# Two query units made in turn, and the count tables merged and loaded earlier, in a one-core graph layer

## The reference

```python
xn = _layernorm(x)                                   # x is 1250 x 1024
x = x + gnn(xn, W, a, src, dst) + mix(xn, w_ql, w_qr, w_key, w_value)
x = x + ffn(_layernorm(x))                           # 8 experts, the best 2 of each row

# gnn: 20000 edges
h = x @ W;  al = h @ a_l;  ar = h @ a_r
e = exp(-leaky_relu(al[src] + ar[dst]))
h_prime = segment_sum(e[:, None] * h[dst], src) / (segment_sum(e, src) + EPS);  elu(h_prime)
# mix
query = (x @ w_ql) * (x @ w_qr)
linear_attn = query @ (key.T @ value)                # key = x @ w_key, value = x @ w_value
```

## Time and profile before

| | us |
|---|---|
| median of 3 runs | 1197.39 |
| the three runs | 1197.3, 1197.39, 1201.2 |
| the profiled execution | 1201.76 |
| its span | 1199.7 |
| PE busy | 1153.2 (96%) |

### The profile page before, as it was taken

One profiled execution on the slowest core, in us unless ns is written; L12 is line 12 of the kernel. 1 busy time (PEld: TensorE's weight loads), 2 busy tenths in 40 slices (PEclk: granted clock), 3 DMA queues, 4 the chain that ended last, 5 costly groups with the idle time before them and its releaser, 6 DMA issues.

```text
span 1199.7 us, 15119 instructions
## 1 busy us (share of the span) xinstructions
PE 1153.2 (96%) x5588; PEld 987.2 (82%) x5588; DVE 586.4 (49%) x1171; ACT 308.7 (26%) x416; POOL 469.8 (39%) x394
## 2 busy tenths in 40 slices
PE   6999999999999999999999989999967999999996
PEld 5898888888788999999978868888855888788884
DVE  7935766655332122211023457978589622644444
ACT  2422112133120221211021223333353411523232
POOL 0003557457787567500000016324323444434343
PEclk9999999999999999999989999999968999999998
DMA  9382875773534445355476653462288954885753
GB/s 356 111 341 53 236 206 115 240 178 51 124 45 43 92 93 118 88 115 117 97 191 186 233 164 112 154 251 102 102 299 295 342 102 92 244 246 121 195 86 72
DMA packets 115835, 192.15 MB, mean 160 GB/s; under 512 B 33960, under 2 KB 63912, under 8 KB 114624
## 3 DMA queue, kind: packets, MB, share of 16 engines
q1 hardware_dynamic: 81008, 159.53, 38.5%
q0 software_dynamic: 34768, 31.82, 19.4%
HBM read 136.19 MB, written 61.68 MB: 165 GB/s over the span
## 4 chain that ended last, share of the span: by engine, by line
PE 80%; DVE 9%; DMA 8%; issue 1%; ACT 1%; SPq 0%; DVEq 0%; POOL 0%; ACTq 0%; POOLq 0%
PE ps L1562 25%; PE ps L1563 25%; PE ps L1564 25%; DMA xm<-in_x 6%; DVE e_lo L1387 2%; PE ps L1781 2%; PE ps L1710 2%; PE ps L1650 1%; DMA gx<-xn_d,tok_of 1%; DVE xn_lo L1114 1%; DVE stats L1086 1%; DVE xm L1311 1%; DVE acc L1102 1%; PE ps L1608 1%; SPq L623 0%
## 5 line engine op out<-in xcount | busy, mean ns | idle before, releaser
L731 POOL DMA_INDIRECT cnt_d<-times,addr_i x160 | 263.2, 1645 | 179.2 <-DMA cnt_d<-times,addr_i 96.5
L1562 PE MATMUL ps<-e_hi,lt_hi 128*128 128x512 f32 x368 | 147.3, 400 | 2.8 <-DVE e_lo L1387 1.9
L1564 PE MATMUL ps<-e_hi,lt_lo 128*128 128x512 f32 x368 | 143.6, 390 | 0.0
L1563 PE MATMUL ps<-e_lo,lt_hi 128*128 128x512 f32 x368 | 143.4, 390 | 0.0
L1563 PE MATMUL ps<-xt_lo,q_hi 128*128 128x416 f32 (+1 forms) x384 | 135.0, 352 | 0.0
L1562 PE MATMUL ps<-xt_hi,q_hi 128*128 128x416 f32 (+1 forms) x384 | 134.9, 351 | 0.0
L1564 PE MATMUL ps<-xt_hi,q_lo 128*128 128x416 f32 (+1 forms) x384 | 134.7, 351 | 0.0
L840 POOL DMA_INDIRECT out<-y,row_put x46 | 74.2, 1613 | 86.7 <-ACT y L1044 49.2
L1562 PEld LDWEIGHTS ps<-e_hi,lt_hi 128*128 128x128 f32 x368 | 69.1, 188 | 23.3 <-DVE e_lo L1387 9.2
L1255 DVE TENSOR_TENSOR qs<-ps,qs 128x416 f32<-128x416 f32 (+1 forms) x24 | 14.2, 592 | 143.4 <-PE ps L1564 143.4
L1562 PE MATMUL ps<-h_hi,att_hi 128*128 128x512 f32 (+1 forms) x200 | 79.6, 398 | 3.7 <-issue 3.7
(11 more groups left out here) (257 smaller groups left out, 2384.4 us busy)
## 6 DMA issues: line engine op xcount, KB each, us to landing
e_raw<-in_L_ffn_expert_W SPq DMA_DIRECT2D x64, 512.0 KB, 9.4
cnt_d<-zeros SPq DMA_DIRECT2D x20, 640.0 KB, 12.8
rows<-key_d SPq DMA_DIRECT2D x8, 1250.0 KB, 7.3
acc<-in_x SPq DMA_DIRECT2D x18, 512.0 KB, 7.8
w_raw<-in_L_mix_w_key SPq DMA_DIRECT2D x16, 512.0 KB, 3.8
cnt_d<-cnt_d POOLq DMA_DIRECT2D x10, 640.0 KB, 7.5
cnt<-cnt_d SPq DMA_DIRECT2D x10, 640.0 KB, 6.5
h_d<-hs SPq DMA_DIRECT2D x18, 256.0 KB, 2.0
```

The costliest lines, as they stand in the source:

```text
L731: nc.gpsimd.indirect_dma_start(out=cnt_d[i], out_offset=bass.IndirectOffsetOnAxis(ap=addr_i[:, j:j + 1], axis=0), in_=times[:, j:j + 1], i ...
L1562: nc.tensor.matmul(o, lh, rh, start=(k == 0), stop=False)
L1563: nc.tensor.matmul(o, lh, rl, start=False, stop=False)
L1564: return nc.tensor.matmul(o, ll, rh, start=False, stop=(k == last_k))
```

## The change

It does four things.

- `Q_SEQ` gives the order of the thirds. Units 0 to 13 stay as they were; those of units 14 and 15 are made in turn: (14,0), (15,0), (14,1), (15,1), (14,2), (15,2).
- The load of query tile 0 follows product (15,0) as before, which now is made three thirds sooner in PE's order. The load of tile 1 follows the store of product (15,1) and waits for third (14,2), since it writes the buffer that unit 14 is still read from.
- The merges wait for thirds (9,0), (9,1), (10,0), (10,1) ... (13,1), two for each unit. Before, merge t waited for the first third of unit 9 + t (t up to 6) and then for the first job of MIX tile 0, 1, 2.
- The loads of count tiles 0 and 1 move from MIX tile 5 to MIX tile 2.

```diff
-    MERGE_Q = 7
+    MERGE_Q = 9
...
-        phase("Q", (["act"] * 3 + ["dve"] * 3) * KB)
+        Q_SEQ = [(i, c) for i in range(NQ - 2) for c in range(3)] + [(NQ - 2 + x, c) for c in range(3) for x in range(2)]
+        phase("Q", [("act", "dve")[i % 2] for i, _ in Q_SEQ])
...
         def q_job(i, c):
-            return first["Q"] + 3 * i + c
+            return first["Q"] + Q_SEQ.index((i, c))
...
                     if i == NQ - 1 and c == 0:
                         load_tile(0)
+                    if i == NQ - 1 and c == 1:
+                        sp.wait_ge(s_full, q_job(NQ - 2, 2) + 1)
                         load_tile(1)
...
             for t in range(NT):
-                if t == NT // 2:
+                if t == 2:
                     sp.wait_ge(s_both, 16 * NT)
...
             for t in range(NT):
-                n = NQ - MERGE_Q + t
-                pool.wait_ge(s_full, 1 + (q_job(n, 0) if n < NQ else mix_job(n - NQ, 0)))
+                pool.wait_ge(s_full, 1 + q_job(MERGE_Q + t // 2, t % 2))
...
-            for i in range(NQ):
+            for i, c in Q_SEQ:
+                lo, w = QC[c]
                 pe.wait_ge(s_qlo, i + 1)
-                for c, (lo, w) in enumerate(QC):
-                    n = q_job(i, c)
-                    bank_free(n)
...
+                n = q_job(i, c)
+                bank_free(n)
```

More of the change, by code:

```diff
@@ L1679, in _ @@
                         x_transposes(both_parts(XT_ORDER[XT_AHEAD + t]))
-            for i in range(NQ):
+            for i, c in Q_SEQ:
+                lo, w = QC[c]
                 pe.wait_ge(s_qlo, i + 1)
-                for c, (lo, w) in enumerate(QC):
-                    n = q_job(i, c)
-                    bank_free(n)
[L1686 to L1689, removed]
+                n = q_job(i, c)
+                bank_free(n)
+                for k in range(KB):
+                    last = three(ps[:, n % NB, 0:w], q_hi[i % 3][:, k, :], q_lo[i % 3][:, k, :],
+                                 xt_hi[:, k, lo:lo + w], xt_lo[:, k, lo:lo + w], k, KB - 1)
+                last.then_inc(s_full, 1)
             pe.wait_ge(s_kvlo, 2 * UNITS)
```

## The result

The changed kernel takes 1190.56 us (median of 5 runs, 1190.14 to 1192.22) against 1197.39 (5 runs, 1197.22 to 1201.2): ratio 0.9939, 95% interval 0.9918 to 0.9960, so 0.6% faster. The prediction was 1188, range 1184 to 1194.5, right in its range and 2.6 us too low.

What follows compares the result with a forecast made beforehand. PE was taken as busy nearly throughout, losing 6.3 and 5.0 us at two stops. Subtracting 11.3 us gave 1190.5 from the profiled execution or 1186.1 from the median; it took 1188 us, range 1184 to 1194.5.

Steps and rivals of the forecast that it cites:

- The first stop: PE idle 3.43 us between Q and MIX, waiting for `q_lo` of query tile 0; closing it saves 6.3 us.
- The second stop: PE idle 3.69 us between MIX and GNN, waiting for `h_lo` of tile 9; closing it saves 5.0 us.
- The lag from the count loads: In MIX, DVE's residual add of job 5 comes 2.4 us behind PE; gone by job 9.
- The rate of 0.61 us a round: In MIX, an undisturbed residual round is 0.61 us shorter than PE's job, so a lag shrinks by that each round.
- The 11.3 us: Total saving from closing both PE stops, at the start of MIX and before GNN: 6.3 plus 5.0 us.
- The 2.85 and 1.29 us: Extra costs added to PE's idle times of 3.43 us before MIX and 3.69 us before GNN.
- I take the middle: For the whole kernel, 1188 us chosen between 1190.5 from the profiled execution and 1186.1 from the median.
- the first of the two branches: The 4.4 us between profiled execution and median sits in the two stops, so closing them gives 1190.5 us.
- The residual loads: Rival, chance 0.12: MIX rounds keep averaging 5.63 us, GNN starts at 714.6; 1194.0 or 1198.4 us.
- only the first stop closes: Rival, chance 0.11: a lag of some 4 us survives at job 18 before GNN; 1195.5 or 1191.1 us.
- The starvation of PE inside MIX: Rival, chance 0.05: a lag from 9.0 us makes PE stop in MIX; three or more stops make it slower.

Runs made afterwards that it cites:

- e2_merge: Kernel before with only the merges moved into units 9 to 13; order of thirds and count loads unchanged: 1191.34 us, ratio 0.9950.
- e8_before_third: Kernel before, unchanged, run once more for a third profile: 1200.56 us (one time).
- e5_turn_count_early: Changed kernel with the merges back in their old places, count loads still at MIX tile 2: 1195.22 us, ratio 0.9980.
- e9_turn_again: Kernel before with only the order of the thirds and the load of query tile 1 changed, a repeat run: 1194.63 us, ratio 0.9967.
- e10_changed_again: Changed kernel, unchanged, run again for more times and a second profile: 1190.91 us, ratio 0.9938.
- e7_tile1_later: Kernel before with only the load of query tile 1 put behind the store of product (15,1): 1197.14 us, ratio 0.9999.
- e4_before_again: Kernel before, unchanged, run again for a second profile and more times: 1196.98 us, ratio 0.9997.

## Why the prediction was right

The mechanism held for the profiled execution, piece by piece; the size of the usual gain was off by 2.6 us.

**The first stop.** Predicted closed, the cast from 595.0, MIX from 598.9: measured 594.60 and 598.5, both 0.4 sooner because PE came to the end of Q 0.4 us sooner. That ACT's copy of (14,2), and no transfer, would come last was right. What I had not worked out is that the late issue and the merge were each necessary: I counted the merges in Q as worth nothing for this stop, and `e2_merge` shows that they close it alone but for 0.37 us.

**The second stop.** Predicted closed, job 18's add at 702.3, GNN from 707.7, `h_lo` 9 in 1.2 us: measured 702.22, 707.45, 1.23. `h_lo` 9 took 2.55 us in the earlier trace rows, where POOL's sums had begun at 714.47, and 2.55 again in `e8_before_third`, `e5_turn_count_early` and `e9_turn_again`, where they had begun before it too (711.41, 711.04, 707.80), but 1.22 to 1.23 in the eight profiles where they had not. That the overlap alone makes the difference is not shown: the `h_lo` of tile 8 in `e9_turn_again` took 1.22 us (707.83) with a sum of POOL from 707.80 to 711.83 beside it. Job 0's add came at 604.9, not 607.5: its residual load was issued at 601.57 rather than 602.8 and took 3.3 us rather than the 4.7 I gave it. The lag from the count loads was 1.4 us at job 5 instead of 2.4, and gone at job 11, not 9, since two more rounds were slow. These two loads landed 5.9 and 6.9 us after their issue. The rate of 0.61 us a round is an average of unequal rounds: in six of the seven profiles with merges in MIX the lag fell by 2.0 to 2.7 us from job 16 to job 18 alone, in `e9_turn_again` by 0.7.

**The sum and its base.** The 11.3 us against the profiled execution is the step that needed the experiments. It was right for that execution (span 11.4 us less), and nearly so in its parts: MIX begins 3.85 us sooner (predicted 3.43), from there to the start of GNN are 6.71 us less (2.85 + 3.69 = 6.54), and the rest is 0.85 us shorter (1.29). The 2.85 and 1.29 us are what the 14 and 8 matmuls behind the two stops took beyond 105.92 / 467 = 0.227 us each; over the first 12 us of GNN the second comes to 1.6, and behind the first stop of `e8_before_third` there was no such loss (clock 1.00). What was off is the step from there to the median: "Nothing shown tells these apart. I take the middle". The kernel before has the second stop only in some of its executions (two of the three profiled) and the low clock behind the first only in some (two of three), and the change removes both stops, so the end is near 1190 wherever one starts from. The times agree: beside `e10_changed_again`, 17 times of the kernel before lie between 1194.48 and 1202.78, the changed kernel's between 1190.05 and 1192.97. That was the first of the two branches, 1190.5, and the measured median is 1190.56. That it fits to 0.1 us is in part luck, as the stretch behind the stops alone moves by 1.6 us or more between executions of one kernel. The middle between a right branch and a wrong one was not a likely value.

Which pieces a usual execution of the kernel before has is not shown, since none at its median was profiled. The nearest is `e7_tile1_later`, whose times are those of the kernel before: profiled at 1196.71, it had the first stop alone and spanned 6.4 us more than the changed kernel, 4.8 of them before GNN.

**The rivals.** The residual loads did not stay the bound, and "only the first stop closes" did not happen. Both are what the profile of `e9_turn_again` shows, so they belong to the merges in MIX, not to the changed kernel. The starvation of PE inside MIX needed, by the prediction's estimate, a lag over 9.0 us; the 7.6 us of the kernel before (job 11) made no stop, and `e5_turn_count_early` reached 11.6 and starved. A third residual buffer was not tried.

**What stays open.** Why the clock fell behind one stop of 3.43 us and not behind another of 3.47 was not varied. Why it stays low for longer in some executions between GNN and the experts was not either. And why a lag of 4 us at job 3 is worked off by job 18 in one execution and grows to 5.0 in another is not shown; the two profiles of the turn alone differ in the lengths of many residual rounds.

## What to carry to other kernels

A profile is one execution. Where a stop hangs on a transfer with another beside it, take a second profile of the same kernel before summing: here a stop of 3.69 or 4.73 us plus the clock (0.53 and 0.54 behind them) was in two of three. Ask of each closed stop which conditions made it; if it needs two, one edit is enough and the gains don't add. An edit that moves traffic away can do more for the longest times than for the shortest, so look at the range of the times as well as their median: with the turn in both, the shortest times are 1.2 us apart and the longest 7.3 (1191.21 to 1200.25 in 12 runs of `e9_turn_again`, 1190.05 to 1192.97 in 6 of `e10_changed_again`). And run each edit alone: moving the merges, one of the four, gives the whole gain as far as these times can tell.

## What was unexpected of the hardware

- Of the stops around and in MIX, the length did not decide what the clock did. It fell behind stops of 3.00 us (`e5_turn_count_early`, 0.50 from 716 to 718 us), 3.16 (`e7_tile1_later`, 0.50 from 603 to 605), 3.43 and 3.69, 4.25 (`e4_before_again`, 0.50 from 604 to 606), 4.73 (`e8_before_third`, 0.54 from 718 to 720) and 5.37 (`e9_turn_again`, 0.50 from 713 to 717), but behind 3.47 us (`e8_before_third`) it stayed at 1.00. It stayed there behind 0.37 (`e2_merge`) and 2.70 us (`e5_turn_count_early`) too. The price of a fall lay between 1.6 and 2.9 us: in the first 12 us of GNN PE made 47 matmuls in the kernel before, 41 in `e9_turn_again` and 54 in the changed kernel, 0.222 us each.
- The fall came once when PE was already at work again: in `e8_before_third` GNN's first matmul took 0.47 us (715.98), from the third on (716.59) 0.63; the granted clock was 1.00 from 714 to 716 us and 0.61 from 716 to 718.
- A 512 KB load took 6.9 us with a 640 KB accumulating transfer beside it and 4.0 without (`e2_merge`), with the next tile's load behind it both times. In `e4_before_again`, with that transfer issued at 589.70, the load took 4.7 us, but SP issued it, at 595.62, only 5.6 us behind the store of product (15,0) (590.06), where the other two profiles of the kernel before have 2.5.
